# Three query products in a row, and the shared u product as three matmuls on rounded parts

## The reference, cut to what matters

```python
q_hk = (hidden_q @ Wq.T).reshape(Bv, Sv, H, K)            # H = 16 heads
q_big = jnp.einsum('bshk,hkq->bshq', q_hk, w_kc_q)        # 192 numbers a head
q_big = _apply_rope(q_big, sin_q, cos_q)
kv_r = _apply_rope(kv_c, sin_k, cos_k)
q_r = jnp.einsum('bshq,hqr->bhsr', q_big, W_qr)
k_r = jnp.einsum('bld,hdr->bhlr', kv_r, W_kr)
scores = jnp.einsum('bhsr,bhlr->bhsl', q_r, k_r)
attn = jax.nn.softmax(scores, axis=-1)
ctx_c = jnp.einsum('bhsl,bld->bhsd', attn, kv_r)
ctx_lat = jnp.einsum('bhsd,hkd->bhsk', ctx_c, w_kc_kv)
return ctx_lat.transpose(0, 2, 1, 3).reshape(Bv, Sv, H * K) @ Wo.T
```

## Time and profile before

| | us |
|---|---|
| median of 3 runs | 379.34 (379.07 to 379.62) |
| profiled execution, its own time | 379.05 |
| profiled execution, span from first to last instruction | 376.8 |
| TensorE busy | 362.0 (96%) |
| VectorE busy | 293.1 (78%) |
| ScalarE busy | 207.2 (55%) |
| GpSimd busy | 174.2 (46%) |

### The profile page before, as it was taken

The page is one execution under the profiler, slowest core; times in us unless marked ns, Lnnn a source line. Parts: engine busy times, 40 slices in busy tenths (PEclk is TensorE's granted clock), DMA queues, the critical chain, the costliest instruction groups (busy, mean ns, idle before and its releaser), DMA issues.

```text
span 376.8 us, 6340 instructions
## 1 busy us (share of the span) xinstructions
PE 362.0 (96%) x2193; PEld 269.1 (71%) x2193; DVE 293.1 (78%) x674; ACT 207.2 (55%) x555; POOL 174.2 (46%) x163
## 2 busy tenths in 40 slices
PE   8899999999999999999999999998999999989996
PEld 8775776777677767876767587864557567779885
DVE  5698698698668786986796656578899988896773
ACT  1524576566647664865575495616975371682240
POOL 2453765486458546754765440581711042146000
PEclk9999999999999999999999999999999999999999
DMA  7639100300301203000004000400000000000101
GB/s 230 237 114 336 77 1 2 111 3 1 114 0 17 96 2 112 3 0 2 0 1 155 2 1 0 124 0 1 2 1 2 0 2 1 0 2 2 40 16 56
DMA packets 9086, 17.53 MB, mean 47 GB/s; under 512 B 2144, under 2 KB 6944, under 8 KB 8160
## 3 DMA queue, kind: packets, MB, share of 16 engines
q1 hardware_dynamic: 9056, 17.14, 13.5%
HBM read 16.09 MB, written 1.05 MB: 45 GB/s over the span
## 4 chain that ended last, share of the span: by engine, by line
PE 67%; DVE 14%; POOL 9%; ACT 4%; issue 3%; DMA 2%; SPq 0%; DVEq 0%; POOLq 0%
PE bank L1523 15%; PE bank L1564 8%; PE bank L1582 7%; PE bank L1573 6%; PE bank L1607 4%; PE bank L1548 4%; POOL prob L463 4%; PE bank L1533 3%; PE bank L1476 3%; PE bank L1827 2%; DVE relu L1159 2%; PE bank L1443 2%; DMA blobs<-in_blob 2%; POOL rot_low L458 2%; PE bank L1444 2%
## 5 line engine op out<-in xcount | busy, mean ns | idle before, releaser
L463 POOL TENSOR_TENSOR prob<-prob,rinv 128x512 f32<-128x512 f32 x64 | 66.0, 1042 | 78.4 <-DVE rinv L1023 78.4
L1523 PE MATMUL bank<-xnT,w 128*128 128x512 f32 x288 | 83.1, 425 | 1.7 <-DVE xnT L920 1.7
L621 ACT ACTIVATE prob<-bank,negmax 128x256 f32<-128x256 f32 x128 | 59.7, 488 | 29.5 <-DVE negmax L1017 29.5
L1017 DVE TENSOR_REDUCE negmax<-bank 128x2 f32<-128x512 f32 x64 | 40.9, 681 | 37.7 <-PE bank L1564 37.7
L1523 PEld LDWEIGHTS bank<-xnT,w 128*128 128x128 f32 x288 | 52.4, 188 | 22.0 <-issue 13.3
L631 ACT COPY probT<-bank 128x512 f32<-128x512 f32 x64 | 35.2, 592 | 23.6 <-PE bank L1573 23.6
L951 DVE TENSOR_TENSOR rot_up<-bank,cb 64x512 f32<-64x512 f32 x64 | 44.1, 689 | 1.6
L458 POOL TENSOR_TENSOR rot_low<-rot_low,rot_up 128x512 f32<-128x512 f32 x32 | 41.0, 1282 | 3.8 <-DVE rot_up L951 3.8
L443 POOL TENSOR_TENSOR c_y<-c_ve,minus_half 128x4 f32<-128x4 f32 (+1 forms) x9 | 9.8, 1087 | 57.8 <-DVE c_ve L901 45.5
L1573 PE MATMUL bank<-ca,prob 128*128 128x128 f32 x256 | 34.2, 273 | 0.3 <-POOL prob L463 0.3
L1573 PEld LDWEIGHTS bank<-ca,prob 128*128 128x128 f32 x256 | 30.1, 140 | 5.3 <-POOL prob L463 0.8
(11 more groups left out here) (212 smaller groups left out, 702.7 us busy)
## 6 DMA issues: line engine op xcount, KB each, us to landing
blobs<-in_blob SPq DMA_DIRECT2D x7, 1024.0 KB, 4.8
xs<-in_x SPq DMA_DIRECT2D x2, 512.0 KB, 4.0
xn<-in_w_fc_t SPq DMA_DIRECT2D x1, 1024.0 KB, 4.9
ctxT<-in_w_proj_t SPq DMA_DIRECT2D x1, 1024.0 KB, 5.4
out<-qk SPq DMA_DIRECT2D x8, 128.0 KB, 1.7
cb<-in_const_b SPq DMA_DIRECT2D x1, 768.0 KB, 8.5
blobs<-in_w_gate SPq DMA_DIRECT2D x1, 704.0 KB, 5.7
blobs<-in_w_up SPq DMA_DIRECT2D x1, 704.0 KB, 7.1
```

The costliest lines, as they stand in the source:

```text
L463: pool.tensor_tensor(p[:], p[:], rinv[:, n % PROBS, :].unsqueeze(2).to_broadcast([P, 2, S]), ALU.mult).then_inc(normed, 1)
L621: ins = act.activation(prob[n % PROBS][:, st, :], pS[n % UNITS][:, st * S:(st + 1) * S], ACT.Exp, bias=negmax[:, n % UNITS, st:st + 1], ac ...
L1017: dve.tensor_reduce(negmax[:, n % UNITS, :], pS[n % UNITS][:].rearrange("p (a s) -> p a s", a=2), AX, ALU.max, negate=True).then_inc(max_r ...
L1523: ins = pe.matmul(q_bank(m)[:], w[a][:, k, r * P:(r + 1) * P], x[b][:, k, c * CH:(c + 1) * CH], start=(i == 0), stop=(i == 5))
```

## The change

The three query products of a round stand in a row, in three banks (0, 4 and 7; bank 4 is that of the contexts too), and the shared u product of round g + 1 stands behind the third. From n = 1 on that product is three matmuls on rounded parts: high x high, high x low, low x high. The high part of `rot_z` is a copy on ScalarE (`rz_round`), the low part a subtraction on VectorE (`rz_rest`, behind the fourth `largest_score`); the weights' parts are made once a pair (`fold_copy` i = 2 and `wqs_low`). On GpSimd the joins all stand behind the fourth `norm_probs`. On ScalarE `u_copy` stands behind the fourth `exponentials`. Waits follow the new banks. In full but for context, the semaphores' declarations and one wait of a late fold:

```diff
@@ -189,2 +189,4 @@
             probT += [part(f"probT_{i}", [P, 2, S], F32) for i in range(2, UNITS)]
+            rz_high, rz_low = part("rz_high", [P, CH]), part("rz_low", [P, CH])
+            wqs = [[part(f"wqs_{j}_{i}", [P, P]) for i in range(2)] for j in range(2)]
@@ -244,3 +246,3 @@
         bank = [ctx.enter_context(nc.psum_tensor(f"bank{i}", [P, 512], F32)) for i in range(8)]
-        pq, pu = [bank[0], bank[7]], bank[2]
+        pq, pu = [bank[0], bank[4], bank[7]], bank[2]
         pS, pV, last_pV = [bank[i] for i in SCORE_BANK], bank[4], [bank[1], bank[3]]
@@ -251,3 +253,3 @@
                 return bank[i] if f == 0 and i < 3 else bank[7]
-            return pu if i < 3 else pq[1]
+            return pu if i < 3 else pq[0]
...
@@ -332,3 +336,3 @@
-            return bank[Q_BANK[m]] if m < QSTEPS else pq[m % 2]
+            return bank[Q_BANK[m]] if m < QSTEPS else pq[m % RT]
@@ -495,8 +499,6 @@
                 norm_probs(UNITS * g + 2)
-                if n < GROUPS:
-                    join(n, 0)
                 norm_probs(UNITS * g + 3)
                 if n < GROUPS:
-                    join(n, 1)
-                    join(n, 2)
+                    for r in range(RT):
+                        join(n, r)
@@ -584,2 +586,3 @@
                 elif i == 2:
+                    act.copy(wqs[f % 2][0][:], pW[:, P:2 * P]).then_inc(wqs_rounded, 1)
                     act.copy(wqk[f % 2][:], pW[:, 0:2 * P]).then_inc(wqk_ready, 1)
@@ -658,2 +661,7 @@
+            def rz_round(n):
+                act.wait_ge(joined, RT * n + 3)
+                act.copy(rz_high[:], rot_z[n % 2][:, 0, :]).then_inc(rz_rounded, 1)
             for g in range(QUIET):
@@ -664,2 +672,3 @@
                     context_copy(g - 1)
+                rz_round(g + 1)
                 exponentials(n)
@@ -667,4 +676,4 @@
                 exponentials(n + 2)
-                u_copy(g + 1)
                 exponentials(n + 3)
+                u_copy(g + 1)
                 turned_probs(n)
@@ -683,2 +692,3 @@
             context_copy(QUIET - 1)
+            rz_round(QUIET + 1)
             exponentials(n)
@@ -1041,2 +1051,19 @@
+            def wqs_low(f):
+                dve.wait_ge(wqk_ready, f + 1)
+                dve.wait_ge(wqs_rounded, f + 1)
+                dve.tensor_tensor(wqs[f % 2][1][:], wqk[f % 2][:, P:2 * P], wqs[f % 2][0][:].bitcast(F32),
+                                  ALU.subtract).then_inc(wqs_parts, 1)
+            def rz_rest(n):
+                dve.wait_ge(rz_rounded, n)
+                if n > 1:
+                    dve.wait_ge(u_ready, 2 * n)
+                dve.tensor_tensor(rz_low[:], rot_z[n % 2][:, 0, :], rz_high[:].bitcast(F32),
+                                  ALU.subtract).then_inc(rz_parts, 1)
+            wqs_low(0)
+            wqs_low(1)
             for g in range(QUIET):
@@ -1044,2 +1071,4 @@
                 first, second = folds_at(g)
+                if g % 2 == 0 and 2 <= g // 2 + 1 < PAIRS:
+                    wqs_low(g // 2 + 1)
                 largest_score(n)
@@ -1049,2 +1078,3 @@
                 largest_score(n + 3)
+                rz_rest(g + 1)
                 rope_straight(m)
@@ -1083,2 +1113,3 @@
             largest_score(n + 3)
+            rz_rest(QUIET + 1)
             inverse_sum(n + 1)
...
@@ -1511,8 +1542,12 @@
                     pe.wait_ge(turned_copied, 2 * c + 2)
-                if m > QSTEPS + 1:
-                    pe.wait_ge(rot_ready, m - 1)
+                if m > QSTEPS + 2:
+                    pe.wait_ge(rot_ready, m - 2)
                     if m % RT == 0 and late_fold_at(m // RT - 2) is not None:
                         pe.wait_ge(wkvo_ready, late_fold_at(m // RT - 2) + 1)
-                elif m == QSTEPS + 1:
+                    if m % RT == 1:
+                        pe.wait_ge(cT_copied, m // RT - 2)
+                elif m == QSTEPS + 2:
                     pe.wait_ge(wkvo_ready, 2)
+                elif m == QSTEPS + 1:
+                    pe.wait_ge(rot_ready, 4)
                 elif m == QSTEPS:
@@ -1531,2 +1566,10 @@
                 pe.wait_ge(joined, RT * n + 2 + shared)
+                if shared and n:
+                    pe.wait_ge(wqs_parts, f + 1)
+                    pe.wait_ge(rz_parts, n)
+                    wh, wl = wqs[f % 2]
+                    pe.matmul(pu[:], wh[:], rz_high[:], start=False, stop=False)
+                    pe.matmul(pu[:], wh[:], rz_low[:], start=False, stop=False)
+                    pe.matmul(pu[:], wl[:], rz_high[:], start=False, stop=True).then_inc(u_ready, 1)
+                    return
                 if shared:
@@ -1589,5 +1632,6 @@
                     pe.wait_ge(kva_ready, 1)
-                    pe.wait_ge(rot_ready, QSTEPS)
+                    pe.wait_ge(rot_ready, QSTEPS + 2)
                 else:
                     pe.wait_ge(cT_copied, g)
+                    pe.wait_ge(rot_ready, min(RT * (g + 2) + 2, ALLQ))
                 pe.wait_ge(probsT_copied, UNITS * g + 2)
@@ -1675,5 +1719,5 @@
                 small_tiles(g)
-                latent_q(m)
+                for r in range(RT):
+                    latent_q(m + r)
                 latent_u(g + 1, 1)
-                latent_q(m + 1)
                 turn_probs(n)
@@ -1691,3 +1735,2 @@
                     pe.matmul(pu[:, P:P + 2], ones, wdiag[:], start=True, stop=True).then_inc(wmax_here, 1)
-                latent_q(m + 2)
                 turn_probs(n + 2)
```

More of the change, by code:

```diff
@@ L273, in build @@
         wqk_ready = sem("wqk_ready")
+        wqs_rounded, wqs_parts, rz_rounded, rz_parts = (sem(n) for n in
+                                                        ("wqs_rounded", "wqs_parts", "rz_rounded", "rz_parts"))
         wkvo_ready = sem("wkvo_ready")
@@ L667, in _ @@
                 exponentials(n + 2)
+                exponentials(n + 3)
                 u_copy(g + 1)
-                exponentials(n + 3)
                 turned_probs(n)
@@ L1471, in prep @@
                 else:
-                    pe.wait_ge(rot_ready, RT * (2 * f - 1) + 5)
+                    pe.wait_ge(rot_ready, RT * (2 * f - 1) + 4)
                 if i < 2:
@@ L1511, in latent_q @@
                     pe.wait_ge(turned_copied, 2 * c + 2)
-                if m > QSTEPS + 1:
-                    pe.wait_ge(rot_ready, m - 1)
+                if m > QSTEPS + 2:
+                    pe.wait_ge(rot_ready, m - 2)
                     if m % RT == 0 and late_fold_at(m // RT - 2) is not None:
                         pe.wait_ge(wkvo_ready, late_fold_at(m // RT - 2) + 1)
+                    if m % RT == 1:
+                        pe.wait_ge(cT_copied, m // RT - 2)
+                elif m == QSTEPS + 2:
+                    pe.wait_ge(wkvo_ready, 2)
                 elif m == QSTEPS + 1:
-                    pe.wait_ge(wkvo_ready, 2)
+                    pe.wait_ge(rot_ready, 4)
                 elif m == QSTEPS:
```

## The result

The changed kernel takes 393.23 us (median of 6 runs, 392.85 to 395.30), the kernel before beside it 379.48 (6 runs, 379.07 to 380.24): ratio 1.0371, 95% interval 1.0346 to 1.0396. The prediction said 392.5, 387.5 to 396.5. The profiled execution took 393.05 us, with a span of 391.2 (before 376.8): +14.4. Around the span lie 1.85 us here and 2.25 before, so the execution's own time grew by 14.0.

A forecast was written before the change was run, and what follows sets the result against it. TensorE's own work was taken to bound the kernel, busy 362.0 of 376.8 us. Start 0.45, joins 4.85, odd rounds 4.1, even rounds 1.0 and round 14 2.88 gave +13.3 on 379.05: 392.35, said as 392.5, range 387.5 to 396.5.

The forecast's parts named there:

- Contention in `rz_rest`: VectorE's subtraction beside GpSimd's first `norm_probs` ends 0.56 us after it, making everything behind it on VectorE 1.09 later.
- The rival without it, 387.9: Rival: no contention in `rz_rest`, VectorE shifts by only 0.60, +8.6 in all, 387.9 us; chance 0.12.
- Joins: In front of rounds 1, 13 and 14 `latent_u` waits for later joins: 1.66, 1.66 and 1.53, together +4.85 us.
- Odd rounds: Rounds 1 to 11: the second fold waits for the first fold's low part from VectorE, 6 x 0.69 = +4.1 us.
- +0.52 for that case: Odd rounds without contention: ScalarE's copy of the first fold ends last, at 9.97, delaying the second fold by 0.52 us.
- Even rounds: Rounds 2 to 10: unit 3 waits for its late `norm_probs`, 5 x 0.20 = +1.0 us.
- Round 14: The shared product waits for VectorE's low part, with no query product between it and the scores: +2.88 us.
- the clock falls: Rival: TensorE's idle time in round 14 drops the clock to 1.2 GHz, two projection groups, +3.5, 396 us; chance 0.03.
- Start: Ahead of the loop: additional 128 x 128 copies stand ahead of ones that TensorE waits for, +0.45 us.
- Saving: Three rounded matmuls cost 0.69 against 0.86 for the float32 shared product: 0.17 us less in each of 15 rounds, 2.6 in all.
- The last step of the forecast: From 392.35 us for the profiled execution to the median, 0.29 above that execution in the kernel before: said as 392.5.

The follow-up runs named there:

- the first join back: The changed kernel with the first join ahead of the fourth `norm_probs` again, as before the change; 397.14 us, ratio 1.0497 to the kernel before.
- the split alone: The kernel before, old order, with the split added, low part on GpSimd: 378.26 us; with the last shared product float32 and weights' high part copied behind `wqk`: 377.80 us.
- the order alone: The changed kernel's order, joins and banks, but every shared product one float32 product, no parts made; 384.98 us, ratio 1.0158 to the kernel before.
- the third query product back: The new order without the split, with the third query product again between the first fold and unit 2's transposes; 381.33 us, ratio 1.0073 to the kernel before.

## Why the prediction was right, point by point

- *Contention in `rz_rest`*: right. The forecast rested on one pair of instructions in the earlier trace rows. Measured were 1.17 beside GpSimd, 0.69 away from it, and the end 0.56 behind GpSimd's. The rival without it, 387.9, is excluded.
- *Joins*: right, 4.42 for 4.85. The times on GpSimd are those predicted. The earlier trace rows already had a join wait of 0.41 in round 0, and its stall grew to 1.80. The order accounts for 0.39 of each and VectorE's shift for 1.1.
- *Odd rounds*: right in place, 0.78 for 0.69. The fold starts when predicted (t = 10.14), but the contexts start 0.87 behind its start and not 0.76 as in the earlier trace rows (from 132.53 to 133.29, in the same timeline): the restart behind a wait costs 0.1, which I had counted in round 14 and not here. VectorE's shift is not its only cause: with the low part on GpSimd, VectorE waits 0.93 for ScalarE's copy and the odd rounds still have +0.59, where the prediction had +0.52 for that case.
- *Even rounds*: mis-sized, 0.09 for 0.20. I took the times of round 7, an odd round; in the next even round the fourth `norm_probs` ends at t = 9.00 (149.13 + 1.04 - 141.17), not at 9.13.
- *Round 14*: the step "+2.88" is right for the stall (+2.94 in each of the three profiles in which the clock stayed up there). What failed is the chance of 0.03 for the rival *the clock falls*: none of the 10 executions of the change had a granted clock of 1.0, one fall being 3.4 x 0.5 / 391 = 0.004 of it. Its price was twice too high: I had two groups of projections, +3.5 (by my own 1.89 a group it should have been +3.8), and it came to 1.67 in all, since the clock was back after 3.4 us. No row of before could exclude it. The Trainium skill, page "TensorE: Matmul & The Clock Gate", section "HAM oscillation — how this bites in real kernels", warns that waits between groups of matmuls can throttle the array again. The change's trace agrees, with 3.06 us of wait and a granted clock of 0.63 and 0.51 behind it, but in the run with the first join back the same wait had 1.00 behind it.
- *Start*: mis-sized, 0.24 for 0.45. Of it 0.17 is seen on TensorE's wait, 0.63 here and 0.46 in the earlier trace rows; the rest is within what the start varies.

```profile
32.12 0.65 PE L1518 MATMUL bank<-blobs 128*64 128x256 f32 x4 [0.63 <-ACT wqk L588]
```

- *Saving*: 0.17 a round is real (0.15 or 0.16 in the even rounds with the split alone). In the change it lies ahead of the waits listed here and shortens no round by itself.
- *The number*: its closeness is in part luck. The terms missed by -0.4 (joins), +0.6 (odd rounds), -0.5 (even rounds), -0.2 (start), +0.1 (stall of round 14) and -0.1 (rest), which together is -0.6. The fall added 1.7 that the sum did not have, and the time around the span took 0.4 off. The last step of the forecast was also rounded low: 392.35 + 0.29 is 392.6, not 392.5.

By cause, from the profiled spans, and in the order in which the experiments add the pieces (another order could share the same sum differently): the order +6.3, VectorE's subtraction +7.6 (3.2 + 1.15 + 0.9 in the rounds up to 13, and 2.95 - 0.59 = 2.4 in round 14), the split on GpSimd -1.4 (-2.0 in rounds 1 to 11, +0.59 in round 14), the fall +1.7, start and rest +0.2: together the 14.4 measured.

## What to carry to other kernels

When one engine is at 96%, an edit that saves work on it wins only as far as the others deliver: here 2.6 us of matmuls were saved and the rounds still came out 12.5 us longer, the fall of the clock left aside. The same split in the old order, its extra subtraction put on the engine with room and its last product left in float32, took 1.5 us less than before, 1.0 of it in the rounds. Before moving a piece of TensorE work, ask what it covered (the product between the folds hid a copy and a subtraction). Place a VectorE instruction with two SBUF inputs where GpSimd is idle: two places further ahead took the change from 393.2 to 387.6 us here.

## What the runs showed of the hardware that was not expected

- A fall to 1.2 GHz of 3.4 us behind a wait of 3.06 us of TensorE, and in two other kernels at a wait of 1.79, in kernels whose TensorE is busy for 94% of the span. Behind dense matmuls it costs 1.67 us, and executions of one kernel differ by it: the change took 392.70 to 393.25 us where the mean clock was 0.996, and 394.02 to 395.30 where it was 0.991 or 0.989.
- VectorE's subtraction of 128x512 with two SBUF inputs, started second, ends 0.56 us after GpSimd's instruction, whether that is a join or a `norm_probs`. Three maxima out of PSUM beside GpSimd's subtraction took 1.89 together, as without it.
- GpSimd's instruction can be the one that gets longer. In round 14 of the change a `norm_probs` that starts together with VectorE's `xn` takes 1.60 and not 1.04 (timelines of GpSimd and VectorE):

```profile
227.94 1.60 POOL L467 TENSOR_TENSOR prob<-prob,rinv 128x512 f32<-128x512 f32 x1 [0.70 <-DVE rinv L1033]
```

```profile
227.94 0.69 DVE L1047 SCALAR_TENSOR_TENSOR xn<-bf_m,xn 128x512 f32<-128x512 bf16 x1
```

- Behind a wait, the six matmuls of the second fold took 0.87 until the next group instead of 0.76, in the change and in the order alone. With the third query product back, without a wait, they took 0.76.
